# Turning the attention probabilities with two DMA transposes per head instead of TensorE identity matmuls

## Time and profile before

| | |
|---|---|
| time, median of 3 runs | 1677.62 us (1675.75 to 1682.42) |
| profiled execution, from its first to its last instruction (span) | 1679.0 us |
| TensorE busy | 1605.5 us, 96% |
| VectorE busy | 1362.1 us, 81% |
| ScalarE busy | 963.5 us, 57% |
| GpSimd busy | 825.8 us, 49% |
| DMA engines, mean over the span | 34 GB/s |

### The profile page before, as it was taken

How to read it: one execution, slowest core, us unless ns; L and a number is a source line. 1 busy time by engine, 2 the same in 40 slices (tenths; PEclk the granted TensorE clock), 3 DMA queues, 4 the chain that set the end, 5 groups by cost and what they waited for, 6 DMA issues and landing times.

```text
span 1679.0 us, 36621 instructions
## 1 busy us (share of the span) xinstructions
PE 1605.5 (96%) x10592; PEld 930.3 (55%) x10592; DVE 1362.1 (81%) x2724; ACT 963.5 (57%) x2391; POOL 825.8 (49%) x961
## 2 busy tenths in 40 slices
PE   4799999999999999999999999999999996999998
PEld 2465555555555555555555555555555553444543
DVE  7788888888878887888788878887888889767744
ACT  3566666666666666666666666666666663322321
POOL 4466555555555555555555555555555552101100
PEclk9899999999999999999999999999999998899999
DMA  7105100000000000000000000000000000010100
GB/s 243 51 27 117 36 27 26 28 26 26 26 28 26 26 26 28 26 26 26 28 26 26 26 27 27 26 26 27 26 27 26 1 6 28 19 45 20 38 26 25
DMA packets 25964, 57.59 MB, mean 34 GB/s; under 512 B 2784, under 2 KB 4544, under 8 KB 25792
## 3 DMA queue, kind: packets, MB, share of 16 engines
q1 hardware_dynamic: 23328, 51.07, 9.5%
q0 software_dynamic: 2464, 4.23, 1.4%
HBM read 55.32 MB, written 4.19 MB: 35 GB/s over the span
## 4 chain that ended last, share of the span: by engine, by line
PE 90%; DVE 5%; issue 2%; DMA 1%; POOL 1%; ACT 1%; SPq 0%; DVEq 0%; POOLq 0%; ACTq 0%
PE ps_p L685 8%; PE ps_t L739 8%; PE ps_p L686 8%; PE ps_p L687 8%; PE ps_p L709 7%; PE ps_p L710 6%; PE ps_o L752 4%; PE ps_o L754 4%; PE ps_o L753 4%; PE ps_s L722 4%; PE ps_s L723 4%; PE ps_s L724 4%; PE ps_s L914 3%; PE ps_s L915 3%; PE ps_p L928 2%
## 5 line engine op out<-in xcount | busy, mean ns | idle before, releaser
L407 POOL TENSOR_SCALAR prob<-prob,inv_sum 128x512 f32<-128x512 f32 (+3 forms) x512 | 295.5, 577 | 550.8 <-DVE inv_sum L1021 516.2
L1005 DVE SCALAR_TENSOR_TENSOR y<-ps_p,wo_scale,y 128x512 f32<-128x512 f32 x512 | 371.6, 746 | 89.3 <-PE ps_p L710 80.5
L536 ACT ACTIVATE pt_hi<-ps_t 128x512 f16<-128x512 f32 (+3 forms) x512 | 199.2, 434 | 259.5 <-PE ps_t L739 259.4
L527 ACT ACTIVATE prob<-ps_s,exp_bias 128x512 f32<-128x512 f32 (+3 forms) x512 | 263.2, 529 | 32.7 <-DVE exp_bias L1017 32.6
L685 PE MATMUL ps_p<-x_hi,w_hi 128*128 128x512 f16 x640 | 245.0, 383 | 7.8 <-issue 3.4
L686 PE MATMUL ps_p<-x_lo,w_hi 128*128 128x512 f16 x640 | 244.3, 382 | 0.0
L687 PE MATMUL ps_p<-x_hi,w_lo 128*128 128x512 f16 x640 | 244.0, 381 | 0.0
L1011 DVE TENSOR_REDUCE neg_max<-ps_s 128x1 f32<-128x512 f32 (+3 forms) x512 | 224.8, 481 | 15.1 <-PE ps_s L725 12.7
L1027 DVE TENSOR_TENSOR pt_lo<-ps_t,pt_hi 128x512 f16<-128x512 f32 (+3 forms) x512 | 224.8, 481 | 0.2 <-ACT pt_hi L536 0.2
L397 POOL TENSOR_TENSOR rot<-rot,swap 128x512 f32<-128x512 f32 x160 | 203.8, 1274 | 15.2 <-DVE rot L983 1.4
L394 POOL TENSOR_TENSOR swap<-swap,sin 128x512 f32<-128x512 f32 x160 | 203.4, 1271 | 10.5 <-DMA wo_scale<-o_scales 3.1
(11 more groups left out here) (113 smaller groups left out, 3086.9 us busy)
## 6 DMA issues: line engine op xcount, KB each, us to landing
w_code<-w_codes SPq DMA_DIRECT2D x36, 384.0 KB, 3.1
w_scale<-w_scales SPq DMA_DIRECT2D x36, 384.0 KB, 3.9
o_code<-o_codes SPq DMA_DIRECT2D x35, 256.0 KB, 2.6
swap<-x SPq DMA_DIRECT2D x16, 256.0 KB, 2.6
out<-z SPq DMA_DIRECT2D x16, 256.0 KB, 2.0
ffn_w<-x SPq DMA_DIRECT2D x3, 1024.0 KB, 9.7
ffn_w<-gate_t POOLq DMA_DIRECT2D x1, 1376.0 KB, 10.2
ffn_w<-up_t POOLq DMA_DIRECT2D x1, 1376.0 KB, 15.8
```

What stands on the lines that cost most here:

```text
L407: pool.tensor_scalar(t, t, inv_sum[:, hp, i:i + 1], P_UP, ALU.mult, ALU.mult).then_inc(norm_done, 1)
L527: act.activation(prob[:, hp, P_AT[i]:P_AT[i] + w], ps_s[:, bank, col:col + w], ACT.Exp, bias=exp_bias[:, hp, i:i + 1], scale=SCORE_SCALE, ...
L1005: dve.scalar_tensor_tensor(tile, ps_p[:, bank, :], scale, tile, ALU.mult, ALU.add).then_inc(o_add, 1)
```

## The change

The probabilities of a head are split into fp16 halves before they are turned (`p_hi` on ScalarE, `p_lo` on VectorE, each one instruction of 128 x 1280), and each half is turned by one DMA transpose issued from SyncE. The identity matmuls, `pt_high` and `pt_low` go. `attend` and `ot_high`, `ot_low` and the output tiles come one head later (output tiles of head n-2 in head n). `down_f` is loaded after the attention's weights instead of at the start. The layout of a row of `prob` is permuted, and `attend` runs 18 narrower matmuls over the same columns instead of 12.

```diff
-P_AT = {3: 0, 2: 512, 1: 896, 0: 1152}
+P_AT = {2: 0, 3: 384, 0: 896, 1: 1024}
+RUNS = ((0, ((2, 2), (0, 2))), (1, ((2, 2), (1, 1))), (2, ((2, 2),)), (3, ((3, 1),)))
...
# SyncE
+            def turn(n, hp):
+                after(sp, ot_ps, n - 1)
+                sp.sem_inc(sp_passed)
+                sp.wait_ge(p_hid, n + 1)
+                sp.sem_inc(sp_passed)
+                sp.dma_start_transpose(pt_hi[:, hp, :, :], p_hi[:, :]).then_inc(pt_hi_in, 16)
+                sp.wait_ge(p_lod, n + 1)
+                sp.sem_inc(sp_passed)
+                sp.dma_start_transpose(pt_lo[:, hp, :, :], p_lo[:, :]).then_inc(pt_lo_in, 16)
...
+            def unit(U, r, more=True, last=False):
+                for h in range(HG):
+                    turn(U * HG + h, h % 2)
+                    if h == 0 and more:
+                        load_w(U + 6, r % 2)
+                        load_o(U + 5, (r + 1) % 2)
...
# ScalarE
-                after(act, t_ps, (n - 1) * NG)
+                after(act, p_lod, n - 1)
...
-            def pt_high(n, g):
...
+            def p_high(n, hp):
+                act.wait_ge(norm_done, (n + 1) * TT)
+                after(act, pt_hi_in, 16 * n)
+                act.activation(p_hi[:, :], prob[:, hp, :], ACT.Copy).then_inc(p_hid, 1)
...
-                    pt_high(n, 0)
+                    p_high(n, h % 2)
...
-                    pt_high(n, 1)
-                    pt_high(n, 2)
...
-                    ot_high(n, h % 2)
+                    if not (first and h == 0):
+                        ot_high(n - 1, (h - 1) % 2)
...
# TensorE
+            def attend(n, upar, h, hp, before):
+                pe.wait_ge(pt_hi_in, 16 * (n + 1))
+                pe.wait_ge(pt_lo_in, 16 * (n + 1))
...
-                    transposes(n, h % 2, 0)
-                    transposes(n, h % 2, 1)
...
-                    transposes(n, h % 2, 2)
+                    if h:
+                        attend(n - 1, r, h - 1, (h - 1) % 2, pieces_before(U - 1))
+                    elif not first:
+                        attend(n - 1, 1 - r, HG - 1, 1, 0)
                     out_tile(n, h, 2)
...
-                    attend(n, U, r, h)
...
# after the last unit
-            turn_xn(TT - 2, ps_t[:, 0, :])
-            last_output(0)
-            last_output(1)
-            turn_xn(TT - 1, ps_t[:, 1, :])
-            last_output(2)
-            last_output(3)
+            for nt in range(KT):
+                last_output(HG - 2, nt)
+            turn_xn(TT - 2, ps_t[:, 0, :])
+            attend(UNITS * HG - 1, (UNITS - 1) % 2, HG - 1, 1, 0)
+            turn_xn(TT - 1, ps_t[:, 1, :])
+            for nt in range(KT):
+                last_output(HG - 1, nt)
...
# VectorE
-            def pt_low(n, g):
...
+            def p_low(n, hp):
+                dve.wait_ge(p_hid, n + 1)
+                after(dve, pt_lo_in, 16 * n)
+                dve.tensor_tensor(p_lo[:, :], prob[:, hp, :], p_hi[:, :], ALU.subtract).then_inc(p_lod, 1)
...
-                    pt_low(n, 0)
+                    p_low(n, h % 2)
                     out_tile(h, 0)
                     out_tile(h, 1)
                     if more:
...
                         maxima(n + 1, hp, 2)
                         bias(n + 1, hp)
                     out_tile(h, 2)
-                    pt_low(n, 1)
-                    pt_low(n, 2)
...
```

More of the change, by code:

```diff
@@ L354, in load_res @@
                 sp.dma_start(xres[:, t % 2, :], x[t // TT, (t % TT) * P:(t % TT + 1) * P, :]).then_inc(res_in[t % 2], 16)
-            sp.wait_ge(rot_sum, 5 * UNITS)
-            for t in range(TT):
-                load_res(t)
+            def unit(U, r, more=True, last=False):
[4 more added lines that the diff above has]
+                        load_o(U + 5, (r + 1) % 2)
+                    if last:
+                        if h == 0:
+                            sp.wait_ge(rot_sum, 5 * UNITS)
+                        load_res(h)
+            unit(0, 0)
+            unit(1, 1)
+            with sp.Fori(1, UNITS // 2 - 1) as p:
+                for r in range(2):
+                    unit(2 * p + r, r)
+            unit(UNITS - 2, 0, more=False)
+            unit(UNITS - 1, 1, more=False, last=True)
+            sp.wait_ge(w_prod, UNITS + 4)
+            sp.dma_start(down_f[:, :], down_s.rearrange("(a d) -> a d", a=1).to_broadcast([P, D])).then_inc(sc_in, 16)
             for c in range(NB):
@@ L727, in scores @@
                 mm.then_inc(s_ps, 1)
[L729 to L746, removed]
+            def attend(n, upar, h, hp, before):
+                pe.wait_ge(pt_hi_in, 16 * (n + 1))
+                pe.wait_ge(pt_lo_in, 16 * (n + 1))
                 if h == 0:
-                    pe.wait_ge(piece_dve, pieces_before(U - 1) + 2)
-                for j in range(TT):
-                    o = ps_o[:, j * P:S]
+                    pe.wait_ge(piece_dve, before + 2)
+                for j, runs in RUNS:
                     vh, vl = v_hi[:, upar, j * HD:(j + 1) * HD], v_lo[:, upar, j * HD:(j + 1) * HD]
-                    pe.matmul(o, vh, pt_hi[:, j, j * P:S], start=(j == 0), stop=False)
-                    pe.matmul(o, vh, pt_lo[:, j, j * P:S], start=False, stop=False)
-                    mm = pe.matmul(o, vl, pt_hi[:, j, j * P:S], start=False, stop=(j == TT - 1))
+                    for i, count in runs:
+                        o = ps_o[:, i * P:(i + count) * P]
+                        a = P_AT[i] // P + j
+                        step = (P_AT[i + 1] - P_AT[i]) // P if count == 2 else 1
+                        ph, pl = (part[:, hp, a:a + (count - 1) * step + 1:step, :] for part in (pt_hi, pt_lo))
+                        pe.matmul(o, vh, ph, start=(j == 0 and i == 2), stop=False)
+                        pe.matmul(o, vh, pl, start=False, stop=False)
+                        mm = pe.matmul(o, vl, ph, start=False, stop=(j == TT - 1))
                 mm.then_inc(ot_ps, 1)
@@ L796, in bank_free @@
                 def bank_free():
-                    if first and idx < 5:
-                        pe.wait_ge(piece_dve, len(START))
+                    if first and idx < 10:
+                        pe.wait_ge(piece_dve, len(START) + sum(q[0] in "KVQ" for q in names[:max(0, idx - 1)]))
                         return
```

99 lines of the change are left out of this document (42 added, 57 removed).

## The result

The changed kernel takes 1905.05 us (median; 1899.29 to 1906.5), 1.134 times the kernel before (95% interval 1.1316 to 1.1361). The prediction was 1716 us with a range of 1664 to 1790: the sign was right, the size was not. Predicted were +38 us, measured +227. (The prediction's own bounds of the loop end at 1797, a little above its stated range; that is far from 1905 too.)

A forecast was written before the change was run, and what follows sets the result against it. TensorE, 96% busy, bounded the old kernel; afterwards a four-engine loop of 10.47 us a head, 10.87 with delays after two pieces, would. 1679 + 34 + 4 = 1717 us, 1716 as median; range 1664 to 1790.

The forecast's parts named there:

- The step that decides: VectorE's new order, `p_low(n)` before `bias(n+1)`, closes a loop of waits through four engines: 10.47 us a head.
- the gain of TensorE that turns into idle time: The 141 us of transposes taken from TensorE are not gained but become its idle time.
- the waits listed as evidence: `p_low` waits for `p_high`, `p_high` for `normalise`; TensorE idles before O2 and the first piece.
- the alternation of heads: Distances between two `bias` instructions of about 10.5 and 11.3 us in turn, longer after two pieces.
- the last head's cost at the end: After the last unit, four uncovered output tiles and bare `ot_high`, `ot_low`: some +4 us.
- `p_low`'s term of 1.44 us: `p_low` on VectorE in the loop: 1.52 us, 1.44 to the next instruction, bounds 1.3 and 1.76.
- GpSimd's rotations don't bind: GpSimd's path, 5.10 + 4 x 1.3 + 0.6 = 10.9 us, fits inside the 11.27 of a two-piece head.
- (a): Rival: the DMA transposes bound the head, over about 4.2 us of queue per half; 2573 us; chance 0.17.
- The load's row: A 384 KB load landed in 3.9 us, taken as a transpose's price: 7.8 us for two, hidden.
- The 256-byte packets: Upper DMA bound: 1280 packets a half at 0.109 us on 16 engines, 8.7 us a half, 17.5 a head.
- (b): Rival: `p_low` at two columns a cycle takes 0.75 us, shortening the loop to 9.78; 1629 us; chance 0.08.
- (c): Rival: only the bare loop counts, every head 10.47 to 10.6 us; 1665 to 1685 us; chance 0.13.

The follow-up runs named there:

- the lock away: The changed kernel with `p_low`'s first input read from PSUM, 1803.64 us; or with `p_low` moved behind `bias` instead, 1734.02 us.
- the move: The changed kernel with `p_low` moved on VectorE to behind the next head's `bias` and the add of O2: 1734.02 us, 1.033.
- 1763.8: The changed kernel with FFN weight loads spread, TensorE's loop written out and `p_low`'s first input from PSUM: 1763.82 us, 1.0509.

## Why the prediction was wrong in size

**What held.** The step that decides did: the loop through four engines was closed. With the lock away a unit is 44.5 with `p_low` in the loop, where the prediction had 43.5, and 42.0 with it outside, 70 us in all. In the kernel as changed the loop held the lock's cost too, and the move gave 171 us. So did the gain of TensorE that turns into idle time, the sign, `p_high` (1.24 predicted, 1.266 measured), the waits listed as evidence, the growing wait for `invert` (516.2 to 657.0), the alternation of heads (seen once the lock is gone, 11.6 and 10.7 against 11.3 and 10.5), and the last head's cost at the end: of the span's growth of 218.5 us, 127 x (12.30 - 10.60) = 216 lie in the heads, where `bias` ran from 57.8 to 1620.0, and 2.7 outside, 4 predicted.

**The step that failed first: `p_low`'s term of 1.44 us.** It was sized by `w_lo`, an instruction of the same kind, which came first and so kept its time; that `normalise` beside it took 3.08 instead of 2.41 was in the same trace and not read. Alone `p_low` takes 1.49. In the change it stands beside GpSimd's rotations and takes 2.17 on the mean, up to 2.68. The prediction's range for it, 1.3 to 1.76, was built from durations only, and asked nowhere which instructions of another engine run at the same time.

**The step that failed with it: "GpSimd's rotations don't bind".** The sum had 1.3 each. Delayed by `p_low` they take up to 2.5, and `rope_high` in front of `exps` makes that part of the loop: 262.1 us of waiting. Removing one SBUF input removed both effects, 101 us of the 189 between forecast and result. From the start of `p_low` to the next instruction are about 2.17 - 0.08 = 2.09 in the change and 1.46 with the PSUM input: 0.63 a head, 80 us, which leaves 21 for the rotations and `rope_high`. This split is an estimate.

**Not seen at all:** the FFN weight loads in front of a transpose (one head, 13 us), and the jumps of TensorE's instruction stream (six times 2.3 us, 14 us). Both came off with 29 us in the changed kernel, 40 with the lock gone. The prediction took TensorE's idle time as free and had no term for the places of the jumps: a unit there is 2.8 us over a steady one before, 4.5 after. It named a fall of the clock as a risk: the mean granted clock of the profiled run is 0.97, 0.99 before, and what that costs was not measured.

**Left:** 1763.8 - 1716 = 48 us. A unit is 44.2 in that kernel and not 43.5, 23 us in all; in the changed kernel's next head, which has one piece, the hop from GpSimd to ScalarE takes 0.11 and that from ScalarE to VectorE 0.13, where 0.05 each was taken, and the maxima with `bias` take 1.21, 0.11 more. Six units where jumps were take 2.5 more, 15 us, about the time that VectorE stands there. The prediction had no term for that, though the trace of the kernel before has it: its mean head of 10.60 was over a steady one, 41.8 / 4 = 10.46. The rest is mostly at the two ends.

**The rivals.** (a), the DMAs as bound, fell: a half is issued in 1.34 us and has landed after 3.4, and without transposes a steady unit is as long. The load's row, 3.9 us, was the right neighbour. The 256-byte packets are really that many, q1 went from 23328 to 359200, but their price was wrong: 0.344 x 16 x 1897.5 / 359200 = 0.029 us each, where the prediction took 0.109 from the loads. The figure of 1309 ns a block, from the Trainium skill's "VectorE: DVE Perf Modes", section "The three transpose paths", would be 13 us for the ten blocks of a half; the trace has 3.4, so as a price block after block it does not hold for a whole row block in one transpose. (b) fell: `p_low` alone takes 1.49 us, not 0.75. (c) fell: no steady head of the changed kernel is under 11.7.

## What to carry to other kernels

An instruction's duration belongs to its place: before pricing one that reads two operands from SBUF on VectorE, look at what GpSimd does in that stretch, and move it or feed one operand from PSUM where the data are there. When work leaves the busiest engine, look first for the loop of waits that its order closes, and then for costs that grow once it stands: at a loop jump a unit was 2.8 us longer in the old kernel, and 6.9 in the new one with the loads spread. When writing out one engine's loop, look at which other engine's loop jumps at the same place. The transposes by DMA were good: with `p_low` out of the loop, the order on ScalarE and VectorE mended, the loads spread and TensorE's loop written out, the new scheme is 3.2% faster than the old kernel, and 2.5% faster than the old kernel with its loop written out.

## What the runs showed of the hardware

- A VectorE instruction with two SBUF inputs and one of GpSimd that reads SBUF shut each other out in either order: `p_low` 1.48 to 2.68 us, a rotation 1.26 to 2.58, `normalise` 2.41 to 3.08 behind `w_lo`, 3.48 behind `p_low` and 4.27 behind both. With one input of `p_low` in PSUM neither it nor the rotation grows.
- A DMA transpose of 128 x 1280 fp16 within SBUF takes 1.34 us of SyncE's queue and 3.4 us to land. With two per head, 256 in all, queue q1 takes 34.4% of the DMA engines' time, 9.5% before. Behind the large weight loads the issue takes up to 12.66 us and the landing up to 21.6.
- A jump in TensorE's instruction stream shows as idle time released by "issue", 3.11 and 2.13 us at one jump, followed by a granted clock of 0.50 in the stretch from 826 to 829, and 1.00 again in the one from 832. Writing the loop out gained 35 us at its six jumps in the kernel with idle time, and next to nothing there in the full one. It gained away from them too: 61 and 12 us in all.
- At the same six places VectorE, whose loop has the same length, stands 2.3 to 2.7 us in the four kernels with TensorE's loop written out, in the head shown 3.2 us after its scores are made.
